# A transformer block on one core: slot 0's shifted scores moved ahead of slot 1's transposed maxima where each attention begins, and the loads and waits around them reordered

## What is computed

```python
# layer 0 attention: 16 heads of width 8, a band of 0.1 around the diagonal
q = x @ Wq.T + bq + ocr_bias; k = x @ Wk.T + bk; v = x @ Wv.T + bv
scores = einsum('bhsd,bhtd->bhst', q, k) / sqrt(8) + band
out = einsum('bhst,bhtd->bhsd', softmax(scores), v) @ Wo.T + bo
# layer 1 attention: latent form, causal; folded by the kernel into q, k, v with precomputed weights
attn = softmax(where(causal, einsum('bhql,bkl->bhqk', q_lat, c_kv) / sqrt(8), -inf))
x = x + 0.5 * ffn(norm(x)); x = x + attn(norm(x)); x = x + 0.5 * ffn(norm(x))   # in each layer
```

## Time and profile before

| | |
|---|---|
| median of 3 runs (lowest, highest) | 464.08 us (457.72, 465.1) |
| the profiled execution, its own time | 460.4 us |
| its span, first to last instruction | 458.4 us |
| TensorE matmul busy | 413.9 us (90%) |
| VectorE busy | 348.8 us (76%) |
| ScalarE busy | 284.8 us (62%) |
| GpSimd busy | 298.3 us (65%) |
| mean granted TensorE clock | 0.981 |
| first entrance, second entrance | about 46 to 75 us, 281 to 306 us |

### The profile page before, as it was taken

The page is one execution under the profiler, slowest core; times in us unless marked ns, Lnnn a source line. Parts: engine busy times, 40 slices in busy tenths (PEclk is TensorE's granted clock), DMA queues, the critical chain, the costliest instruction groups (busy, mean ns, idle before and its releaser), DMA issues.

```text
span 458.4 us, 11229 instructions
## 1 busy us (share of the span) xinstructions
PE 413.9 (90%) x3804; PEld 265.9 (58%) x3804; DVE 348.8 (76%) x878; ACT 284.8 (62%) x523; POOL 298.3 (65%) x569
## 2 busy tenths in 40 slices
PE   8999789999999998897879888899999999887996
PEld 3555436666666654454447564567667766544674
DVE  5878766888778766996699986767788878367992
ACT  5886424666676676687886448055547575777732
POOL 5523625777777772357899647245676789779962
PEclk9999988999999999899899999989999999999999
DMA  7001876323224100000000006983343332000001
GB/s 215 2 1 49 203 211 166 107 77 85 88 73 104 55 4 1 2 0 2 0 1 2 1 1 165 234 224 93 80 104 107 82 80 56 5 0 1 23 24 46
DMA packets 31123, 31.82 MB, mean 69 GB/s; under 512 B 4953, under 2 KB 26329, under 8 KB 31074
## 3 DMA queue, kind: packets, MB, share of 16 engines
q1 hardware_dynamic: 31074, 31.18, 25.6%
HBM read 21.30 MB, written 9.44 MB: 67 GB/s over the span
## 4 chain that ended last, share of the span: by engine, by line
PE 49%; DVE 18%; POOL 15%; issue 8%; ACT 8%; DVEq 0%; POOLq 0%; ACTq 0%
PE psum L722 6%; ACT h_sb L349 4%; DVE nm L821 4%; POOL hq L1496 3%; PE psum L672 3%; PE psum L675 3%; PE psum L703 3%; PE psum L693 2%; PE psum L673 2%; POOL hb_v L1491 2%; PE psum L726 2%; DVE xn L240 2%; PE psum L694 2%; PE psum L660 2%; DVE nm L824 2%
## 5 line engine op out<-in xcount | busy, mean ns | idle before, releaser
L771 ACT ACTIVATE h_sb<-psum 128x1024 f32<-128x1024 f32 (+1 forms) x128 | 110.9, 914 | 45.9 <-PE psum L694 25.5
L821 DVE TENSOR_REDUCE nm<-psum 128x2 f32<-128x512 f32 x128 | 81.7, 684 | 15.0 <-PE psum L673 14.5
L824 DVE TENSOR_REDUCE nm<-psum 128x3 f32<-128x384 f32 x128 | 65.6, 551 | 10.8 <-PE psum L679 8.9
L781 POOL TENSOR_TENSOR h_sb<-h_sb,bandw 128x512 f32<-128x512 f32 x45 | 57.2, 1271 | 0.0
L246 POOL TENSOR_TENSOR rstd<-veps,mhalf 128x4 f32<-128x4 f32 (+1 forms) x29 | 27.7, 954 | 39.9 <-DVE veps L232 38.8
L722 PE MATMUL psum<-h_sb,v_b 128*32 128x256 f32 x512 | 40.9, 391 | 3.4 <-POOL h_sb L785 1.7
L785 POOL TENSOR_SCALAR_AFFINE_SELECT h_sb<-h_sb 128x512 f32<-128x512 f32 x64 | 40.8, 637 | 0.0
L672 PE MATMUL psum<-kst,qst 72*128 72x256 bf16 x128 | 33.9, 282 | 2.9 <-DMA kst<-k_dram 1.2
L858 DVE RECIPROCAL rsum<-psum 128x16 f32<-128x16 f32 x32 | 8.2, 256 | 33.7 <-PE psum L738 33.7
L675 PE MATMUL psum<-kst,qst 72*128 72x128 bf16 x128 | 29.1, 227 | 5.0 <-DVE nm L824 3.1
L673 PE MATMUL psum<-kst,qst 72*128 72x256 bf16 x128 | 33.3, 276 | 0.0
(11 more groups left out here) (256 smaller groups left out, 1176.2 us busy)
## 6 DMA issues: line engine op xcount, KB each, us to landing
qst<-q_dram SPq DMA_DIRECT2D x96, 96.0 KB
kst<-k_dram SPq DMA_DIRECT2D x96, 96.0 KB
q_dram<-q_parts SPq DMA_DIRECT2D x16, 192.0 KB, 2.6
k_dram<-k_parts SPq DMA_DIRECT2D x16, 192.0 KB, 2.8
k_dram<-k_parts SPq DMA_DIRECT2D x16, 128.0 KB, 2.9
x<-in_L_attn_x SPq DMA_DIRECT2D x4, 256.0 KB, 4.3
out_x<-x SPq DMA_DIRECT2D x4, 256.0 KB, 2.3
pk<-in_packed SPq DMA_DIRECT2D x1, 689.5 KB, 5.9
```

What stands on the lines that cost most here:

```text
L771: nc.scalar.activation(pexp[p][:, :, 0:w], psum[:, 4 + 2 * (p % 2):6 + 2 * (p % 2), 0:w], ACT.Exp, scale=scale).then_inc(sem("a_exp"), 1)
L781: ins = nc.gpsimd.tensor_tensor(wide, wide, bandw[:].unsqueeze(1).unsqueeze(1).to_broadcast([P, 2, 2, P]), ALU.mult)
L821: nc.vector.tensor_reduce(nm[slot % 2][:, HEAD[h]], bank[e].rearrange("p (t k) -> p t k", t=2), AX.X, ALU.max, negate=True).then_inc(sem(" ...
L824: nc.vector.tensor_reduce(nm3[slot % 2][:, HEAD[h]], bank[e][:, 0:3 * P].rearrange("p (t k) -> p t k", t=3), AX.X, ALU.max, negate=True).t ...
```

## The change

Four things are done.

1. In `front`, slot 1, TensorE makes slot 0's first two pairs of shifted scores ahead of `pe_maxT` of slot 1, and ScalarE the two exponentials ahead of `act_maxT` of slot 1. The first `unit` of a layer leaves them out, and with them one dummy matmul.
2. On SP, the stack of slot 3 is loaded in `prefetch`, directly behind that of slot 2, and no longer in the first `unit`.
3. In layer 1, ScalarE writes the second part of unit 0's keys directly behind that of its queries, ahead of v's copy and unit 1's first parts.
4. In layer 1, TensorE waits for v at slot 1 of `front` and no longer at slot 0. GpSimd's wait stays.

```diff
             def act_body(act, k, par, there):
                 if there(0):
                     xT_act(act, k + (tu0 - p0), par, "p_vps", k - 1, bx)
+                second = k - 1 == p0 and not l0
                 if there(1):
                     act_second(act, k - 1, 1 - par, 0, "q")
+                if second:
+                    act_second(act, k - 1, 1 - par, 1, "k")
                 if there(1) and not l0:
                     act_v(act, k - 1)
                 if there(0):
                     act_first(act, k, par, 0, "q")
-                if there(1):
+                if there(1) and not second:
                     act_second(act, k - 1, 1 - par, 1, "k")
...
                 if which == "sp":
-                    if has_3:
+                    if has_3 and has_prev:
                         sp_stack(eng, *n3)
...
-                    pe_shifted(eng, qd, slot, 0)
-                    pe_idle(eng, opening, 2)
+                    if has_prev:
+                        pe_shifted(eng, qd, slot, 0)
                     if late:
                         pe_y(eng, *yb)
-                    pe_shifted(eng, qd, slot, 1)
+                    if has_prev:
+                        pe_shifted(eng, qd, slot, 1)
...
                 if which == "act":
-                    act_exp(eng, qd, slot, 0)
-                    act_exp(eng, qd, slot, 1)
+                    if has_prev:
+                        act_exp(eng, qd, slot, 0)
+                        act_exp(eng, qd, slot, 1)
...
                     sp_stack(eng, q0, 2)
+                    sp_stack(eng, q0, 3)
...
                 if slot == 0:
-                    for name, v in {"pe": [("p_v", 4 * inst + 4)], "pool": [("p_v", 4 * inst + 4)]}.get(which, []):
-                        eng.wait_ge(sem(name), v)
+                    if which == "pool" or which == "pe" and l0:
+                        eng.wait_ge(sem("p_v"), 4 * inst + 4)
                 if slot == 1 and which == "pe":
+                    if not l0:
+                        eng.wait_ge(sem("p_v"), 4 * inst + 4)
...
                     if slot == 1:
+                        pe_shifted(eng, q0, 0, 0)
+                        pe_shifted(eng, q0, 0, 1)
                         pe_maxT(eng, q0, 1)
...
                 if which == "act":
+                    if slot == 1:
+                        act_exp(eng, q0, 0, 0)
+                        act_exp(eng, q0, 0, 1)
                     act_maxT(eng, q0, slot)
```

## The result

The changed kernel takes 465.61 us (median of 21 runs, 462.79 to 467.94), the kernel before 462.05 us beside it (median of 21, 456.79 to 465.1). The ratio is 1.0111 with a 95% interval of 1.0083 to 1.0138: slower by 1.1%, within the 2% that was called no change, but with the sign against the forecast of 458.3 us and just above its range, which ended at 465.0. The profiled execution took 465.5 us with a span of 463.5, where the one before took 460.4 with 458.4: 5.1 us more.

What follows compares the result with a forecast made beforehand. TensorE was taken to bound the kernel, busy 69.17 of 70 us in the attention loop. Gains of 1.8 + 1.7 + 0.4 = 3.9 us gave 456.5 or 460.2 us, middle 458.3; range 454.0 to 465.0.

Steps and rivals of the forecast that it cites:

- issue at 61.0, landed at 63.5: First entrance, SP's write of slot 0's row: issued 0.6 us later than the old 60.42, landed after 2.50 us.
- issue 295.2, landed at 297.6: Second entrance, slot 0's row: maxima ready at 293.2, issue after unit 1's save at 294.8 plus 0.4 us held.
- The flight: Slot 0's row write, from issue to landing: 2.50 us, read where a weight load waited for one.
- The held issue: SP ahead of slot 0's row, first entrance: delay 0.6 us, between bounds of 0.1 and 2.6 us.
- Rival 2: Both entrances: the row queues behind the fourth stack and lands 2.5 us later; 4.7 us lost, 466.9 us; chance 0.12.
- the queue was nearly empty there: Argument against the row queueing: at the old issue, 60.42, the save had been issued for 2.4 us.
- If the clock holds: First entrance, from slot 2's second pair to the next unit: 5.8 us instead of 7.50 at full clock, 1.7 us gained.
- the two steps of the first entrance: Slot 2's second pair 1.8 us sooner by the new order, then 1.7 us more behind it at full clock.
- The second entrance's order, 0.4 us: Second entrance: transpose, first pair and shifted pairs end at 300.8 against 301.15; bounds 1.7 and -0.6 us.
- Keys and v, 0.67 us: Second projection: sooner keys remove GpSimd's idle 0.67 us, and the later v wait lets the first scores start that much sooner.
- Covered terms: Costs taken as hidden: row 1's later write by 2.4 us, next quad's stack by 1.3, ScalarE's table load 0.
- rival 3: Behind the entrance: SP held 1.3 us or more, next quad's stack late, gain given back; 462.2 us; chance 0.13.

Runs made afterwards that it cites:

- e1: The changed kernel with the fourth stack loaded in the first unit again, behind slot 1's row; ratio 0.9927 to the kernel before.
- e4: The changed kernel with the fourth stack issued directly behind slot 0's row, ahead of unit 2's save; ratio 0.9943 to the kernel before.
- e5: The e4 kernel with unit 0's keys' second part back behind queries' first part in the second projection; ratio 0.9928 to the kernel before.
- e6: The e4 kernel with TensorE waiting for v ahead of slot 0's scores in layer 1 again; ratio 0.994 to the kernel before.
- e11: The e4 kernel unchanged, timed again in five rounds; ratio 0.9915 to the kernel before.
- e12: The e10_row_act_alone kernel with SyncE issuing nothing in this place until slot 0's row has landed; one execution, 462.1 us, no ratio.
- e9_half_ahead: The changed kernel with three of the fourth stack's six transfers ahead of slot 0's row and three directly behind it; ratio 0.9962 to the kernel before.
- e3_row_act: The changed kernel with slot 0's row written from ScalarE's DMA queue, the fourth stack still ahead; ratio 1.0058 to the kernel before.
- e10_row_act_alone: The changed kernel with the fourth stack back in the first unit and slot 0's row written from ScalarE's queue; ratio 1.0029 to the kernel before.
- e13_before_fill: The kernel before with seven more dummy matmuls per entrance ahead of slot 1's transposed maxima, no part of the change; ratio 0.994 to the kernel before.
- e8_second_only: The kernel before with only the sooner keys' second part and the later wait for v in layer 1; ratio 1.0059 to the kernel before.
- e2_stack_only's: The kernel before with only the fourth stack moved behind the third; ratio 1.008 to the kernel before.
- e7: The changed kernel with 14 and 20 dummy matmuls in the holes ahead of slot 0's first shifted scores; ratio 1.0014 to the kernel before.

## Why the prediction was wrong

**What failed: the time at which the row lands.** The step that ends with "issue at 61.0, landed at 63.5", and its copy in the second entrance, "issue 295.2, landed at 297.6". Two terms:

- The flight. I took 2.50 us from a row write in a quiet stretch and used it in a loaded one. It was 4.11 and 4.36 us. Where the fourth stack was not ahead and SyncE's save not beside it, the flight was 2.26 to 2.51 us, in both entrances of e1, e4, e5, e6, e11 and e12. The prediction's upper bound of the row's delay, 2.6 us, counted the transferred bytes only as time for which SyncE is held, and not once more on the flight behind the issue; the measured delay is 1.69 us of issue and 1.61 of flight, 3.3 us.
- The held issue. I took 0.6 us, near the lower end, "since SP was idle 2.4 us ahead of the row". The issue came at 62.11. In the second entrance the issue was right: 296.90 less the 1.66 us by which everything came later is 295.24, against 295.2. There only the flight failed, and the issue was right in part by luck: SyncE was held 1.6 us longer in the save's last pair (2.91 against 1.29), where I had added 0.4, but 1.0 us less in its first pair (1.05 against 2.07), which I had carried over.

The wrong thought behind both: an idle SyncE queue was read as an empty one, and what it held in the kernel before was taken for what it would hold with six transfers more. With nothing more ahead than before it was in fact nearly empty. In e4_stack_behind_row, where the row is issued at 60.48, the DMA share is 0.83 from 60 to 61 and 0.12 from 61 to 62; in the changed kernel it is 1.01 over the whole flight:

```profile
62.11:66.22 4.11, 0.86 (x5) 0.21 (x4) 1.39 (x3) 0.00 (x0) 0.87 (x4) 0.95 1.01 294
```

A busy stretch alone does not make the row late, though. In the second entrance of e1_stack_back the share over the flight is 0.94, with unit 1's save issued until 291.93 and unit 2's directly behind the row, and the row takes 2.48 us:

```profile
292.89:295.37 2.48, 1.89 (x20) 1.05 (x19) 2.29 (x5) 1.27 (x1) 0.00 (x0) 1.00 0.94 272
```

**Rival 2 is what happened**, with a chance of 0.12. It had the row landing at 66.0 (measured 66.2), the second pair of slot 2 at 69.8 (69.95), and in the second entrance at 303.3 (304.77 less 1.66 is 303.1). Its price of 4.7 us compares with 5.1 between the profiles, of which some 0.85 came ahead of the first scores. That the sum is so near is in part luck. It has 2.6 us for the first entrance, where B is only 0.75 us longer, and 2.1 for the second, where 3.45 are lost, with 6.8 us at half clock against 3.4 before, which it did not count; and its flight grows by the bytes ahead, where e9_half_ahead has the full flight with half of them. Its 466.9 us lies within 1.3 of the median. The argument against it, "the queue was nearly empty there", was the one that failed; the rule of the Trainium skill cited then, "DMA: Bandwidth & Descriptors", section "Queues, rings and completion order", pointed the right way. The same section of the Trainium skill says further that a completion count is written only after every earlier write of that DMA engine, across its queues. e3_row_act and e10_row_act_alone agree with it: a row on a queue of its own flew 3.73 to 5.75 us. No run here tells this order of writes from the mere sharing of the DMA engines.

**The clock.** "If the clock holds" was a condition on a hole of about 1.1 us; the hole was 3.25 and the clock fell behind it. With the fourth stack behind the row the condition is met, and the two steps of the first entrance are right in sum: 1.8 + 1.7 = 3.5 us forecast, 3.61 measured by B and 3.50 by the start of the next unit (71.22 against 74.72). Their split was not: by e13_before_fill the clock is 2.75 of it. The stretch that I had put at 1.8 us for the order alone had part of the half clock in it already.

**The second entrance's order, 0.4 us.** Wrong with the row's flight. With the stack behind the row B is 0.70 us shorter (21.43) than in e8_second_only (22.13), which keeps the old order and has the full clock there as well.

**Keys and v, 0.67 us.** Right: 0.63 us in the changed kernel (13.19 from the projection's start to the first scores against 13.82), 0.60 and 0.73 when either is undone. That the wait shown as "ACT v_all" in the earlier trace rows was the stack's was right as well: with the later v wait the bracket reads "DMA kst<-k_dram". The cost at nothing for what ScalarE does later was too low: the last copy of v comes 0.75 us later relative to the projection, which only the later wait hides.

**Covered terms.** GpSimd's idle 0.67 us of the earlier trace rows is gone: its two thirds run at 276.77 and 277.90, back to back (rows in the last section). ScalarE's table load moved into the hole, as forecast beside the earlier trace rows:

```profile
294.58 0.27 ACT L804 ACTIVATE nmT<-psum 48x128 bf16<-48x128 f32 x1 [5.99 <-PE psum L751]
294.87 1.28 ACT L774 ACT_TABLE_LOAD   x1
```

ScalarE's later copy of row 1 cost nothing, and no unit waited for kst behind the entrance in the changed kernel, so rival 3 did not occur there. Its sign does appear once the entrance is fast: the next quad's stack, which I had as covered by 1.3 us, is waited for 0.62 to 1.30 us behind the second entrance of e1, e4, e5, e6, e8 and e11, and 0.89 us behind the first of e6. The fourth stack's old place had a price that I had not named: in e1_stack_back 0.64 and 0.94 us for the unit behind it.

**Left open.** How long the half clock lasts behind a hole of 1.77 us in code that did not change (6.8, 10.2 and 13.7 us in three kernels) is not explained, and between before and e8_second_only it makes some 4 us in the first entrance. Longer holes don't make it longer: behind 2.33 and 2.44 us in e9_half_ahead and e10_row_act_alone it lasted 3.4 us. Nor is it shown what exactly holds the row's flight at 4.0 to 4.6 us on SyncE's queue with half or all of the stack ahead. Verdicts of half a per cent, like e2_stack_only's and e8_second_only's, carry that with them.

## What to carry to other kernels

The flight of a small transfer that an engine waits for, read in a quiet stretch, does not hold when a change puts bulk loads ahead of it or beside it on another queue. Neither an idle issuing queue nor the DMA share of the stretch tells it: here the row took its quiet time at mean shares from 0.31 to 0.94, and nearly twice that once three more stack transfers stood ahead. Put bulk loads that are not yet needed behind the small transfer on its own queue. When an operation is moved ahead of others on an in-order engine, its latest input becomes theirs too, so the arrival of that input has to be priced under the load that the same change makes. And where a hole is followed by half clock, fill it with dummy matmuls once as an experiment: it prices the clock apart from the wait, and here it gave a ratio of 0.994 by itself.

## What the runs showed of the hardware that was not expected

A row write of 12 KB took 2.26 to 2.51 us behind 18 stack transfers and a save, in twelve entrances, while the mean DMA share over its flight went from 0.31 to 0.94. With three or six more stack transfers (288 or 576 KB) ahead on the same queue it took 4.01 to 4.61. From ScalarE's queue, which held nothing else, it took 2.36 and 2.51 with SyncE silent, 4.42 and 3.73 with unit 2's save issued around it, and 5.75 and 5.04 with 576 KB of stack ahead and a save beside it.

In the first entrance the clock fell in every kernel whose last hole was 1.77 us or more (before, after, e2, e3, e8, e9 and e10) and in none where the holes were 0.5 us or less (e1, e4, e5, e6, e11, e12, and the filled e7 and e13). In the second it was less regular: with holes of 1.83 and 1.85 us it held in e2, e8 and e10, and fell in the kernel before. It also fell at about 54 us in e5, e7 and e8, behind holes of 1.33 to 1.52 us ahead of the first scores, where holes from 1.16 to 2.04 us at the same place left it up in the other kernels. So the length of the last hole alone does not decide it.

VectorE's four normalisations in the second projection take 1.10 to 1.12 us with none of GpSimd's third parts beside them. They take 1.94 to 1.95 us before and in e2, e5 and e13, where those for unit 0's queries and keys run with a gap between them, and 2.80 us in every kernel where the two run back to back. Rows of the changed kernel, VectorE and then GpSimd:

```profile
276.33 2.80 DVE L240 TENSOR_SCALAR xn<-x,mv,rstd 128x128 f32<-128x128 f32 x4
```
```profile
276.77 1.17 POOL L503 TENSOR_TENSOR q_parts<-q_r,q_parts 128x512 bf16<-128x512 f32 x1 [2.97 <-ACT q_parts L499]
277.90 1.15 POOL L503 TENSOR_TENSOR k_parts<-k_r,k_parts 128x512 bf16<-128x512 f32 x1
```

TensorE's next transpose waits 0.96 us for it (in the kernel before the same transpose starts at 276.67 with no wait). That the two engines share their access to SBUF is what the Trainium skill's "GPSIMD Engine Reference" says in its table of SBUF interfaces; the cost here, 0.86 us, was hidden, since the stack and not the projection ended the wait.
